# Access patterns of the products and sums in a 32x32 block inverse on VectorE

## The reference

```python
def step(Sm, inp):                      # one token, all heads
    q_, k_, v_, g_, b_ = inp
    Sm = Sm * jnp.exp(g_)[..., None, None]
    kv = jnp.einsum('bhk,bhkv->bhv', k_, Sm)
    delta = (v_ - kv) * b_[..., None]
    Sm = Sm + jnp.einsum('bhk,bhv->bhkv', k_, delta)
    o = jnp.einsum('bhk,bhkv->bhv', q_, Sm)
    return (Sm, o)
...
on = og * jax.lax.rsqrt(var + EPS) * norm_w
return on.reshape(B, S, VAL_DIM) @ w_out
```

## Time and profile before

| | us |
|---|---|
| median of 3 runs | 2325.9 |
| lowest and highest | 2322.84, 2326.07 |
| span of the profiled execution, first to last instruction | 2332.5 |
| PE busy in it | 2129.5 (91%) |
| DVE busy | 1837.5 (79%) |
| ACT busy | 1510.2 (65%) |
| POOL busy | 900.0 (39%) |

### The profile page before, as it was taken

One profiled execution on the slowest core, in us unless ns is written; L12 is line 12 of the kernel. 1 busy time (PEld: TensorE's weight loads), 2 busy tenths in 40 slices (PEclk: granted clock), 3 DMA queues, 4 the chain that ended last, 5 costly groups with the idle time before them and its releaser, 6 DMA issues.

```text
span 2332.5 us, 48904 instructions
## 1 busy us (share of the span) xinstructions
PE 2129.5 (91%) x18108; PEld 1760.5 (75%) x18108; DVE 1837.5 (79%) x3536; ACT 1510.2 (65%) x3585; POOL 900.0 (39%) x760
## 2 busy tenths in 40 slices
PE   4559999999999999999999999999887899999998
PEld 4448888888888888888887888887776466666677
DVE  6889798888979888897989889797324767767665
ACT  4546767767676776767776676765566766566632
POOL 1543444435344443534454354433234122323232
PEclk8779999999999999999999999999888999999999
DMA  3322312222231322223232322311243012221232
GB/s 75 89 71 50 87 35 77 57 64 65 47 88 33 78 56 67 65 46 78 44 78 52 70 63 47 77 23 54 58 142 132 1 46 91 93 97 47 100 131 95
DMA packets 274635, 161.54 MB, mean 69 GB/s; under 512 B 209352, under 2 KB 246752, under 8 KB 269280
## 3 DMA queue, kind: packets, MB, share of 16 engines
q1 hardware_dynamic: 274400, 158.41, 26.0%
HBM read 122.43 MB, written 35.91 MB: 68 GB/s over the span
## 4 chain that ended last, share of the span: by engine, by line
issue 35%; PE 25%; POOL 21%; DVE 11%; ACT 4%; DMA 2%; SPq 1%; POOLq 0%; DVEq 0%; ACTq 0%
POOL EB L494 4%; POOL SM L576 4%; PE ps L1703 4%; PE ps L1325 3%; POOL EB L498 3%; PE ps L1327 3%; PE ps L1326 3%; POOL SM L583 2%; PE ps L1450 2%; POOL Q L554 2%; POOL WL L472 2%; POOL SZ L578 2%; DVE A L897 1%; PE ps L1615 1%; ACT SC L844 1%
## 5 line engine op out<-in xcount | busy, mean ns | idle before, releaser
L897 DVE SCALAR_TENSOR_TENSOR A<-ps,CW,A 128x508 f32<-128x508 f32 (+2 forms) x768 | 515.9, 734 | 119.3 <-ACT A L669 114.5
L571 POOL TENSOR_SCALAR SM<-SM 128x8 f32<-128x8 f32 x64 | 12.6, 197 | 899.0 <-ACT DL L688 899.0
L1325 PE MATMUL ps<-XH,WH 128*128 128x512 f32 x512 | 220.2, 430 | 51.0 <-DVE A L897 49.9
L1450 PE MATMUL ps<-WO,DL 128*128 128x256 f32 x1008 | 244.7, 395 | 8.9 <-ACT TTF L799 8.9
L1450 PEld LDWEIGHTS ps<-WO,DL 128*128 128x128 f32 x1008 | 190.2, 195 | 42.6 <-ACT DL L675 14.1
L1327 PE MATMUL ps<-XH,WL 128*128 128x512 f32 x512 | 205.9, 402 | 0.0
L1326 PE MATMUL ps<-XL,WH 128*128 128x512 f32 x512 | 205.7, 402 | 0.0
L688 ACT ACTIVATE DL<-SZ 128x128 f32<-128x128 f32 x512 | 152.3, 298 | 72.2 <-issue 49.0
L1114 DVE TENSOR_TENSOR SZ<-SZ,ps 128x512 f32<-128x512 f32 x128 | 86.4, 686 | 131.3 <-PE ps L1484 131.3
L844 ACT ACTIVATE SC<-ps,A 128x128 f32<-128x128 f32 x512 | 141.7, 386 | 51.8 <-DVE A L1230 51.2
L1099 DVE TENSOR_TENSOR BP<-ps,EB 128x512 f32<-128x512 f32 x256 | 158.3, 681 | 4.1 <-ACT EB L663 4.1
(11 more groups left out here) (221 smaller groups left out, 5846.7 us busy)
## 6 DMA issues: line engine op xcount, KB each, us to landing
EB<-decay_rows SPq DMA_DIRECT2D x128, 256.0 KB, 4.7
WE<-expert_halves SPq DMA_DIRECT2D x32, 1024.0 KB, 5.2
x_blocks<-BP SPq DMA_DIRECT2D x256, 32.0 KB, 1.6
X<-x_blocks SPq DMA_DIRECT2D x16, 512.0 KB, 6.2
tt_blocks<-TI SPq DMA_DIRECT2D x16, 512.0 KB, 2.6
tn_blocks<-TM SPq DMA_DIRECT2D x16, 512.0 KB, 2.6
TTF<-tt_blocks SPq DMA_DIRECT2D x256, 32.0 KB, 1.9
expert_halves<-BP SPq DMA_DIRECT2D x8, 1024.0 KB, 5.7
```

What stands on the lines that cost most here:

```text
L897: dve.scalar_tensor_tensor(acc, ps(i, 0, [[128, 4], [1, 128 - s]]), at(CW, tile * 4 + 3 - s, [[1, 1]]), acc, ALU.mult, ALU.add).then_inc(s ...
L1325: pe.matmul(out, sa, ma, start=(kt == 0), stop=False)
L1450: t = pe.matmul(ps(7 - i, b * 256, [[1, 256]]), at(on_buf(k), (4 * i + 2 * b + v) * 128, [[1, 128]]), at(WO, (k // 4 % 2) * 512 + v * 256, ...
```

## The change

The three loops of `inverse(j)` keep their instructions, their order, their number, their element counts and the estimates for `pump`. What changes is the order in which the elements of each are visited. The multiplies put the summed index second to last in `TM`, so that the index of the output column is innermost. Of the operands of a multiply one is then read along a row (inner step 1), the other repeats each element (inner step 0), and `TM` is written with step 1. The sums read `TM` with an inner step of s (s = 2, 4, 8) or 16, over s or `kn` elements. L954's output is written along rows where it was written down columns; `UT` for s = 2, 4, 8 is stored by rows. For s = 2, where the loop runs over one index inside each block, it now runs over the output row, not over the output column, so offsets change too.

```diff
                     for s in (2, 4, 8):
                         nb, blk = 16 // s, 66 * s
+                        mid = ([s * s, nb * s], [1, s], [s, s])
...
-                                dims = ([[s * s, s], [s, s], [1, s]], [[1, s], [0, s], [32, s]], [[0, s], [32, s], [1, s]])
+                                dims = ([[s * s, s], [s, s], [1, s]], [[0, s], [32, s], [1, s]], [[32, s], [1, s], [0, s]])
                             else:
-                                o, xo, to = it * s * s, s + it, 0
-                                dims = ([[s ** 3, nb], [s, s], [1, s]], [[blk, nb], [0, s], [32, s]], [[blk, nb], [32, s], [1, s]])
+                                o, xo, to = it * s * s, s, it * 32
+                                dims = ([[s ** 3, nb], [s, s], [1, s]], [[blk, nb], [32, s], [1, s]], [[blk, nb], [1, s], [0, s]])
...
-                        dve.tensor_reduce(at(UT, 0, [[1, nb * s * s]]), at(TM, 0, [[s, nb * s * s], [1, s]]), AX.X, ALU.add,
+                        dve.tensor_reduce(at(UT, 0, [[1, nb * s * s]]), at(TM, 0, mid), AX.X, ALU.add,
                                           negate=False).then_inc(inv, 1)
...
-                                dims = ([[s * s, s], [s, s], [1, s]], [[1, s], [0, s], [32, s]], [[0, s], [1, s], [s, s]])
+                                dims = ([[s * s, s], [s, s], [1, s]], [[0, s], [32, s], [1, s]], [[s, s], [1, s], [0, s]])
...
-                        dve.tensor_reduce(at(TI, s, [[blk, nb], [1, s], [32, s]]), at(TM, 0, [[s, nb * s * s], [1, s]]),
+                        dve.tensor_reduce(at(TI, s, [[blk, nb], [32, s], [1, s]]), at(TM, 0, mid),
...
-                        dve.tensor_tensor(at(TM, 0, [[16 * kn, 4], [kn, 16], [1, kn]]), at(X, k0 * 32 + 16, [[0, 4], [1, 16], [32, kn]]),
-                                          at(TI, k0 * 32 + k0, [[32, 4], [0, 16], [1, kn]]), ALU.mult).then_inc(inv, 1)
+                        dve.tensor_tensor(at(TM, 0, [[16 * kn, 4], [16, kn], [1, 16]]), at(X, k0 * 32 + 16, [[0, 4], [32, kn], [1, 16]]),
+                                          at(TI, k0 * 32 + k0, [[32, 4], [1, kn], [0, 16]]), ALU.mult).then_inc(inv, 1)
...
-                        dve.tensor_reduce(at(UT, k0, [[1, 4], [16, 16]]), at(TM, 0, [[kn, 64], [1, kn]]), AX.X,
+                        dve.tensor_reduce(at(UT, k0, [[1, 4], [16, 16]]), at(TM, 0, [[16 * kn, 4], [1, 16], [16, kn]]), AX.X,
                                           ALU.add).then_inc(inv, 1)
```

More of the change, by code:

```diff
@@ L944, in inverse @@
                                 o, xo, to = it * s ** 3, it * blk + s * 33, it * s * s
-                                dims = ([[s * s, s], [s, s], [1, s]], [[1, s], [0, s], [32, s]], [[0, s], [1, s], [s, s]])
+                                dims = ([[s * s, s], [s, s], [1, s]], [[0, s], [32, s], [1, s]], [[s, s], [1, s], [0, s]])
                             else:
-                                o, xo, to = it * s * s, s * 33 + it, 0
-                                dims = ([[s ** 3, nb], [s, s], [1, s]], [[blk, nb], [0, s], [32, s]], [[s * s, nb], [1, s], [s, s]])
+                                o, xo, to = it * s * s, s * 33, it * s
+                                dims = ([[s ** 3, nb], [s, s], [1, s]], [[blk, nb], [32, s], [1, s]], [[s * s, nb], [1, s], [0, s]])
                             dve.wait_ge(inv, done)
@@ L972, in inverse @@
                         dve.wait_ge(inv, done)
-                        dve.tensor_tensor(at(TM, 0, [[16 * kn, 4], [kn, 16], [1, kn]]),
-                                          at(TI, 16 * 32 + 16 + i0, [[1, 4], [0, 16], [32, kn]]),
-                                          at(UT, 0, [[0, 4], [1, 16], [16, kn]]), ALU.mult).then_inc(inv, 1)
+                        dve.tensor_tensor(at(TM, 0, [[16 * kn, 4], [16, kn], [1, 16]]),
+                                          at(TI, 16 * 32 + 16 + i0, [[1, 4], [32, kn], [0, 16]]),
+                                          at(UT, 0, [[0, 4], [16, kn], [1, 16]]), ALU.mult).then_inc(inv, 1)
                         done += 1
@@ L978, in inverse @@
                         dve.wait_ge(inv, done)
-                        dve.tensor_reduce(at(TI, 16 + i0, [[1, 4], [32, 16]]), at(TM, 0, [[kn, 64], [1, kn]]), AX.X,
+                        dve.tensor_reduce(at(TI, 16 + i0, [[1, 4], [32, 16]]), at(TM, 0, [[16 * kn, 4], [1, 16], [16, kn]]), AX.X,
                                           ALU.add, negate=True).then_inc(inv, 1)
```

## The result

| | before | changed |
|---|---|---|
| median of 4 runs, us | 2325.99 | 2288.52 |
| lowest and highest | 2322.84, 2329.91 | 2284.63, 2292.52 |
| span of the profiled execution | 2332.5 | 2282.7 |

The ratio is 0.9835, with a 95% interval from 0.9804 to 0.9867: 37.5 us less, in the stated range, 20 us short of the forecast. The two profiled executions overstate it: that of before was above the timed ones, that of the changed kernel the lowest of four, so the spans are 49.8 us apart, 12.3 more than the medians.

A forecast was written before the change was run, and what follows sets the result against it. DVE was taken to bound one iteration in four, PE the rest. 44.8 us (long iteration), 8.7 (clock drops) and 4 (first inverse) made 57.5 us, so 2325.9 - 57 = 2269; own range 2251 to 2285, widened to 2250 to 2300.

The forecast's parts named there:

- the lengths of products and of L967: Sign: products near 0.69 us for 512 elements and 1.22 for 1024; the 16-term sum of 1024 (then L966) at 1.94.
- the iterations at 24.2 to 25 us: Sign: the iterations of 28.4 us, with the s = 8 part of the inverse, fall to 24.2 to 25.
- the wait before `gate` near zero: Sign: PE's waits for L897, L1114 and L1109 from 200 to 1500 us come near zero.
- The bound: DVE bounds one iteration in four, the one with the s = 8 part of the inverse; PE bounds the rest.
- Products and their repeated operand: Multiplies of the inverse: a repeated operand costs nothing extra, 1.04 ns an element; 0.69 us for 512, 1.22 for 1024.
- The path in the long iteration: s = 8 iteration: block ends 4.4 us earlier, `gate` begins 3.65 earlier, PE's 3.2 us wait goes; 14 rounds, 44.8 us.
- Iterations 4j+7: Shorter products and longer sums together under 1 us either way, inside DVE's spare 1 to 6 us; no gain counted.
- Clock drops: After the long iteration: all six drops to a lower clock go, 1.45 us each, 8.7 us.
- The first inverse: Start of the run, DVE the bound: instructions on TM, 34.35 us, get 4 us less (bounds 0 and 7).
- The first (L583 holds L950): Rival: in the long iteration POOL's L583 keeps L950 waiting, `gate` 1.8 us later than forecast; 2292, chance 0.10.
- A step of 8: Rival that short steps cost more than long ones: sums at 2.5 ns an element, 2320 us; chance 0.12.
- The slower rival: POOL's L578 gets in before L934's second part, block ends 0.55 us later than now; 2344, up to 2364; chance 0.08.

The follow-up runs named there:

- e1: Changed kernel with the old patterns back in the two 16-term loops, so new patterns for s = 2, 4, 8 only: 2316.2 us, ratio 0.9930.
- e7: Kernel before, old access patterns, with the same three-instruction move out of the iteration that DVE bounds: 2283.2 us, ratio 0.9842.
- e2: Kernel before with the new patterns in the two 16-term loops only: 2330.0 us, ratio 0.9988.
- e3: Changed kernel with every TENSOR_REDUCE reading adjacent elements (inner step 1), which makes the inverse a different one: 2252.2 us, ratio 0.9660.
- e6: Changed kernel with three inverse instructions moved from the iteration that DVE bounds into the one in front of it: 2268.9 us, ratio 0.9773.
- e4: Changed kernel with POOL's L554 squaring 8 elements in place of 512 from the second group on: 2324.6 us, ratio 0.9969.
- e8: Changed kernel with three inverse instructions moved one iteration ahead, and old patterns for s = 2 and 4: 2265.5 us, ratio 0.9768.

## Why the prediction was right, and where it was not

**The number** owes part of its rightness to the margin. 2288.5 lies outside the range of the forecast itself (2251 to 2285) and inside the one widened for a rival that didn't happen. Part of the 20 us is a wrong step outside the kernel: the sum was made for the profiled execution and its difference taken for that of the medians. Between the profiled executions it was 49.8 for 57.5; 12.3 us are lost because the profiled execution of the kernel before lies above that kernel's median and that of the changed one below its own. Of the signs, the lengths of products and of L967 came out; the iterations at 24.2 to 25 us (25.76), the wait before `gate` near zero (11.6) and no drop of the clock (one) did not.

**The bound** was read rightly: DVE in one iteration of four, PE elsewhere. The experiments with one half of the change each, and the one with the sums read flat, show it by the iteration lengths.

**Products and their repeated operand:** 0.69 and 1.22 us, as taken.

**The path in the long iteration** is the term that was mis-sized: 14 x 2.6 = 36 us for 44.8. The steps up to L951's first part came out in the order given. `gate` began 20.7 us after the iteration's start, 2.6 earlier than before, not 3.65. Of the missing 1.07, L554 between the parts of L951 is 0.7: I had put L951's second part 0.1 us ahead of it. The rest is the price of the s = 8 sums, L939 2.16 for 1.94 and L955 2.10 for 1.94: I took one rate from a 32-step read for all steps, and sums with step 8 are at 1.9.

**Iterations 4j+7** were costed at nothing, "inside DVE's spare", and gave 6.5 us. That about as much was gained here as the long iteration fell short of its 44.8 was luck. What I left out is who else waits for these products: POOL's L578 took 3.27 us there before and 2.94 now, L576 2.87 and 2.30, so POOL's decay rows (L498), ACT's exponentials (L663) and then the copies (L812) that PE waited for are earlier. In the kernel before, ACT waits for the first of these and PE for the last, once a round:

```profile
ACT EB L663 <- POOL EB L498: 7.0, 13, 0.6
```

```profile
PE ps L1584 <- ACT DL L812: 4.1, 13, 0.4
```

Both waits are there with the old patterns of the 16-term loops (before, e1, e7), and both are absent with the new ones (the changed kernel, e2, e3, e6). POOL's timeline before and in the changed kernel:

```profile
752.50 2.87 POOL L576 TENSOR_TENSOR SM<-SM 128x8 f32<-128x8 f32 x1
755.44 3.27 POOL L578 TENSOR_TENSOR SZ<-SZ,SM 128x1024 f32<-128x1024 f32 x1
```

```profile
832.78 2.30 POOL L576 TENSOR_TENSOR SM<-SM 128x8 f32<-128x8 f32 x1
835.16 2.94 POOL L578 TENSOR_TENSOR SZ<-SZ,SM 128x1024 f32<-128x1024 f32 x1
```

The links between weren't varied one by one. PE's wait is 0.3 of the 0.5 us; PE is also busy for 0.2 less in this iteration (24.44 for 24.62), which stays open.

**Clock drops:** "all six go" was wrong twice. A recount of the before profile gives five, not six; and one stays after the change, because a stall of 0.8 us stays and some drops follow it. How many do varies: one or two of 14 in the changed kernel's profiles, nine in e1's with 0.8 us of stall, ten in e4's with 2.0, six in e2's and five in the kernel before with 3.2. So the number doesn't grow with the stall. In the runs with no stall in 4j+5 (e3 and e8 in all rounds, e6 and e7 from the second) there is none after it. Of the changed kernel's four timed runs the fastest has a mean granted clock of 0.968 and the slowest 0.964, which fits that these drops, 1.45 or 3.0 us each, make much of the spread; it isn't shown. How often they come was not settled.

**The first inverse** was to gain 4 us and lost 2: DVE's instructions on TM take 36.17 us for 34.35. (The window of the earlier trace rows would cut the last sum, which ends at 151.48 us; in the kernel before all end by 149.5, so the longer window gives 34.35 there too.)

```profile
97.00:166.00 69.00, 36.17 (x38) 0.63 0.29 58
```

Its products take 20.5 us together for 24.2, its sums 15.6 for 10.2. The sums pay in full; undisturbed, the products would save about as much (an estimate from 1.74 and 1.88 ns an element before and 1.04 now), but several wait for POOL streams for longer than before (L974 with 1024 elements takes 2.56 us here, 1.23 undisturbed). My bounds, 0 to 7 gained, excluded a loss for no reason.

**The rivals.** The first (L583 holds L950), at 2292 the nearest in time, is not what happened: L951 ran beside L583 undisturbed. Something else, L554, took that place with half the price. A step of 8 does cost more than one of 16 (1.72), but 1.9 ns, not 2.5, and a step of 4 costs 1.75. The slower rival's race, with L578, was won by 0.19 to 0.27 us in all 14 rounds. e4 shows what such a lost race costs: 14 x 1.1 = 15 us for 0.02 us, without the drops of the clock that followed.

## What to carry to other kernels

Before you shorten instructions on an engine that shares something with another, write both timelines side by side: here 3.1 of the 3.45 us won in the critical block were waits that an order of arrival had caused, and moving three instructions in the old kernel bought as much as rewriting the access patterns. An index made innermost for one operation becomes a stride for the next; count both, by elements. And look for spare time in the neighbouring iteration before you make the full one faster.

## What the runs showed of the hardware

- A multiply with two SBUF inputs and a POOL stream take turns, and who waits goes next; a sum with one SBUF input runs beside POOL. (The s = 8 sums vary from 2.00 to 2.16 us; L955 takes 2.10 with POOL idle, so POOL isn't shown to be the reason.) POOL instructions on 4 or 8 elements, 1.0 and 1.6 us long, held no product for more than 0.1 us, though a product does hold them: L576 takes 1.65 us alone and took 2.87 behind L973 in the kernel before.
- The Trainium skill (SBUF — State Buffer, "Who interferes with whom") calls the pair of ports that VectorE and GpSimd share an exclusive lock, and says that whoever issues first has it for the whole instruction while the other blocks. For streams the trace agrees; for the small instructions the 0.69 us of L951 begun inside L583 decide against it.
- A stepped read by TENSOR_REDUCE costs, per element: 1.75 to 1.77 ns at step 4, 1.9 at step 8, 1.72 at step 16, for 1.04 at step 1 (158 ns fixed taken off). An inner step of 0 costs nothing, at 692 ns for 512 as for contiguous operands.
